# Where the score shifts of three of four token groups are computed in a cross-attention kernel, and by which engines and queues they reach their consumer

## The chip, the cores and the metric

One core of one Trainium2 chip runs the whole program. The metric is device time in microseconds (us) of one execution; beside it stands the span of the profiled execution, from its first to its last recorded instruction. The kernel works in float32 throughout; where speed matters it splits a float32 operand into an upper and a lower float32r part and multiplies the parts.

## The reference, cut to what matters

```python
# x: (16, 100, 512), ctx: (16, 722, 256); B, T, E = 16, 100, 512; M, L = 722, 256
q = x @ Wq + bq
k = ctx @ Wk + bk
v = ctx @ Wv + bv
w = softmax((q @ k.T) / sqrt(E), axis=1)      # over the 100 tokens t, not over the context rows
y = w @ v + x
out = (y - mean(y)) * rsqrt(var(y) + 1e-6) * gamma + beta
```

The softmax runs over the tokens. A score of token t and context row m is ctx[m]·G[t] plus a term that depends on the token alone, c[t] = x[t]·u + bb, with u = Wq·bk and bb = bq·bk, both scaled by 1/sqrt(E). Because the softmax is over t, this term, the score shift, cannot be left out.

## The kernel before, in words

The 16 batches are dealt with in four groups of four (400 tokens each). The start computes W = Wq·Wk (transposed) and u on TensorE from weights loaded in four parts, and then project(g) forms G for the 400 tokens of group g. From then on each batch b passes through a turn: scores_of(b) (24 matmuls into ps_S, lines 417 to 421), maxima(b) on VectorE (add the shift to the scores, then the negated maximum over tokens, lines 744 and 748), exponentials(b) on ScalarE, normaliser(b) on VectorE, probabilities(b) on GpSimd, weighted_ctx(b) (24 matmuls into ps_U, line 433), and then, for tiles of 128 output rows, values, residual and layer norm.

Every engine runs its instructions in the order written. TensorE's order is written out at lines 471 to 487: project(0), project(1), scores of batch 0, project(2), scores of 1, project(3), then turns in which scores_of(b) comes ahead of weighted_ctx(b - 2). scores_of(b) waits for S_read, that is for maxima(b - 1) to have emptied the single pair of score banks. weighted_ctx(0) waits also for the G of all four groups, the last of which ScalarE takes (take_group(3)) after exponentials(1).

The shift of a group is made in this way. VectorE multiplies the transposed tokens xT_in (feature on the partition, 400 tokens along the row) by u, one feature chunk after another: weigh_by_u, four instructions of 128x400 (lines 724 and 728). ScalarE (upper_shift, line 567) and VectorE (lower_shift, line 735) split the result. TensorE (sum_shift, lines 407 and 408) multiplies both parts by a matrix of ones, which sums over partitions and leaves the sum on all 128 of them; ScalarE (take_shift, line 571) copies it into c_rows, from which maxima reads. Nothing of it touches a DMA queue.

VectorE's order is written out at lines 827 to 869. After maxima(0) come lower_half(3) (line 715, the lower part of group 3's tokens), weigh_by_u(1), normaliser(0), maxima(1), chunk_sum(0), normaliser(1), lower_shift(1), weigh_by_u(2), maxima(2), and so on.

The loads all go through SyncE's one queue (lines 265 to 318). It issues the weights, the four groups of tokens, two batches of context in both layouts, three parameter rows, Wv and two tiles of x without a wait, and then waits in turn for buffers: next_ctxT(2) waits for the scores of batch 0 and next_ctx(2) for weighted_ctx(0). There are two buffers each for ctxT and ctx.

Of the kernel before, what the change touches and what calls it, by code (L numbers as in the profile page):

```python
# [24 lines left out]
P = 128  # L25
# [5 lines left out]
def xattn(nc, xT, x, ctxT, ctx, Wqk, Wv, bv, gamma, beta, out):  # L31
# [18 lines left out]
    with ExitStack() as stack:  # L50
        def sb(name, shape, dt=F32):
            return stack.enter_context(nc.sbuf_tensor(name, shape, dt))
# [4 lines left out]
        def sem(name):  # L57
            return stack.enter_context(nc.semaphore(name))
# [12 lines left out]
        g_bias = sb("g_bias", [P, LC])  # L71
# [16 lines left out]
        xu_hi = sb("xu_hi", [P, 2, GT], F32R)  # L88
        xu_lo = sb("xu_lo", [P, 2, GT], F32R)
# [49 lines left out]
        u_set = sem("u_set")  # L139
        gbias_set = sem("gbias_set")  # L140
# [58 lines left out]
        y = wv_in  # L199
        centred = wqT[:, 0:2, :]  # L200
# [16 lines left out]
        def tile_of(b):  # L217

            return next((j for j in range(NT) if last_batch(j) == b), None)
# [44 lines left out]
        def _(sp):  # L264
# [65 lines left out]
        def _(pe):  # L330
# [35 lines left out]
            def bias_sums():  # L366

                pe.wait_ge(wkq_step, EC)
                for c in range(LC):
                    last = nc.tensor.matmul(ps_w[:, c:c + 1], wkq[:, (EC - 1) % 2, c * P:(c + 1) * P], ones[:, 0:1],  # L370
                                            start=True, stop=True)
                last.then_inc(gbias_summed, 1)
# [26 lines left out]
            def sum_shift(g):  # L399

                pe.wait_ge(xuhi_set, g + 1)
                pe.wait_ge(xulo_set, g + 1)
                if g >= 1:
                    pe.wait_ge(c_set, g)
                else:
                    pe.wait_ge(onesr_set, 1)
                nc.tensor.matmul(ps_c[:, 0:GT], ones_r[:, :], xu_hi[:, g % 2, :], start=True, stop=False)  # L407
                nc.tensor.matmul(ps_c[:, 0:GT], ones_r[:, :], xu_lo[:, g % 2, :], start=False, stop=True).then_inc(c_summed, 1)  # L408
# [65 lines left out]
            sum_shift(0)  # L474
# [4 lines left out]
            sum_shift(1)  # L479
# [65 lines left out]
        def _(act):  # L545
# [17 lines left out]
            def upper_shift(g):  # L563
                act.wait_ge(xu_step, EC * (g + 1))
                if g >= 2:
                    act.wait_ge(c_summed, g - 1)
                nc.scalar.activation(xu_hi[:, g % 2, :], xu[:, (EC - 1) % 2, :], ACT.Copy).then_inc(xuhi_set, 1)

            def take_shift(g):
                act.wait_ge(c_summed, g + 1)  # L570
                nc.scalar.activation(c_rows[:, g * GT:(g + 1) * GT], ps_c[:, 0:GT], ACT.Copy).then_inc(c_set, 1)
# [63 lines left out]
            nc.scalar.activation(g_bias[:, :], ps_w[:, 0:LC], ACT.Copy, scale=SCALE).then_inc(gbias_set, 1)  # L635
# [3 lines left out]
            upper_shift(0)  # L639
            take_group(1)  # L640
            upper_half(3)
            take_shift(0)
            exponentials(0, 0)
            take_group(2)
            upper_shift(1)
# [5 lines left out]
            upper_shift(2)  # L651
            upper_U(0, 0)
            exponentials(2, 0)
            take_shift(1)
            value_bias(0)
            exponentials(3, 1)
            turn(4, 0)
            turn(5, 1)
            take_shift(2)
            each_turn(turn, 6, 9)  # L660
            upper_shift(3)
            turn(9, 1)
            turn(10, 0)
            take_shift(3)
            each_turn(turn, 11)
# [20 lines left out]
        def _(dve):  # L686
# [32 lines left out]
            def weigh_by_u(g, terms=tuple(range(EC))):  # L719
                if g >= 1 and 0 in terms:  # L720
                    dve.wait_ge(xulo_set, g)
                for e in terms:
                    if e == 0:
                        nc.vector.tensor_scalar(xu[:, 0, :], xT_in[:, g, 0, :], u_col[:, 0:1], bb_col[:, 0:1],
                                                ALU.mult, ALU.add).then_inc(xu_step, 1)
                    else:
                        dve.wait_ge(xu_step, EC * g + e)
                        nc.vector.scalar_tensor_tensor(xu[:, e % 2, :], xT_in[:, g, e, :], u_col[:, e:e + 1],  # L728
                                                       xu[:, (e - 1) % 2, :], ALU.mult, ALU.add).then_inc(xu_step, 1)

            def lower_shift(g):
                dve.wait_ge(xuhi_set, g + 1)
                if g >= 2:
                    dve.wait_ge(c_summed, g - 1)
                nc.vector.tensor_tensor(xu_lo[:, g % 2, :], xu[:, (EC - 1) % 2, :],
                                        xu_hi[:, g % 2, :].bitcast(F32), ALU.subtract).then_inc(xulo_set, 1)

            def maxima(b, q):
                dve.wait_ge(c_set, b // GB + 1)
# [87 lines left out]
            weigh_by_u(0)  # L827
            lower_half(2, (0,))
            lower_shift(0)
# [5 lines left out]
            weigh_by_u(1)  # L835
# [4 lines left out]
            lower_shift(1)  # L840
            weigh_by_u(2)
            maxima(2, 0)
            lower_U(0, 0)
            lower_shift(2)
# [15 lines left out]
            turn(5, 1)  # L860
            weigh_by_u(3, (0, 1))
            turn(6, 0)
            weigh_by_u(3, (2,))
            turn(7, 1)
            weigh_by_u(3, (3,))
            turn(8, 0)
            turn(9, 1)
            lower_shift(3)
            each_turn(turn, 10, B - 1)
# [181 lines left out]
```

## Time and profile before

| | us |
|---|---|
| runs, median (lowest to highest) | 143.87 (143.75 to 144.3) |
| the profiled execution's own time | 144.33 |
| its span | 142.6 |
| TensorE matmul busy | 135.5 |
| VectorE busy | 114.1 |
| ScalarE busy | 78.7 |
| GpSimd busy | 65.2 |

Busy times count the records of an engine. TensorE's loads of weights lie beside its matmuls. The profile's granted clock of TensorE over the run is 0.991 of full speed. The DMA queue of SyncE moved 34.79 of 37.33 MB.

### The profile page before, as it was taken

How to read it: one execution, taken by the hardware profiler on the slowest of the kernel's cores; microseconds unless marked ns; L12 is line 12 of the kernel's file. 1: busy time of each engine (PE TensorE's matmuls, PEld its weight loads, DVE VectorE, ACT ScalarE, POOL GpSimd, SP SyncE). 2: the span in 40 equal slices, each digit the busy share in tenths (PEclk: the TensorE clock that was granted, in tenths of full speed). 3: DMA queues.
4: the chain of work that ended last, by engine and by line, in shares of the span. 5: the costliest groups of instructions: out<-in, count | busy, mean ns of one | idle time of the engine just before them, and what ended most of it. 6: DMA issues, size and time to landing. Idle time of an engine off the chain costs nothing.

```text
span 142.6 us, 2971 instructions
## 1 busy us (share of the span) xinstructions
PE 135.5 (95%) x1046; PEld 130.9 (92%) x1046; DVE 114.1 (80%) x221; ACT 78.7 (55%) x282; POOL 65.2 (46%) x61
## 2 busy tenths in 40 slices
PE   6999999999999999989999999999999999999940
PEld 6899999999998999989999999999999999999930
DVE  0379995996997779689999987877789976797993
ACT  4167088577276924574655638474847546386320
POOL 1000000027304681734667553639486645639991
PEclk9999999999999999999999999999999999999996
DMA  4999999936077595986996979697997985635314
GB/s 148 333 397 419 423 300 381 353 156 214 11 260 255 172 390 159 353 342 163 340 319 241 334 259 375 225 336 229 303 305 247 341 291 219 219 114 183 138 43 178
DMA packets 10814, 37.33 MB, mean 262 GB/s; under 512 B 1200, under 2 KB 1456, under 8 KB 10800
## 3 DMA queue, kind: packets, MB, share of 16 engines
q1 hardware_dynamic: 9424, 34.79, 69.8%
q10 hardware_dynamic: 1376, 2.36, 4.4%
q8 instruction: 8, 0.13, 0.4%
q14 instruction: 6, 0.05, 0.1%
HBM read 33.87 MB, written 3.28 MB: 260 GB/s over the span
## 4 chain that ended last, share of the span: by engine, by line
PE 88%; POOL 6%; issue 2%; ACT 1%; DVE 0%; POOLq 0%; DVEq 0%
PE ps_S L419 29%; PE ps_U L433 26%; PE ps_Y L454 10%; PE ps_U L392 6%; PE ps_Y L392 6%; PE ps_Y L337 3%; POOL xT_in L970 2%; POOL xT_in L958 2%; PE ps_S L341 1%; POOL prob L947 1%; PE ps_w L442 1%; PE ps_U L341 1%; PE ps_c L407 1%; POOL rstd L963 1%; PE ps_c L408 1%
## 5 line engine op out<-in xcount | busy, mean ns | idle before, releaser
L578 ACT ACTIVATE expo<-scores,negmax 121x100 f32<-121x100 f32 x96 | 35.0, 366 | 28.4 <-DVE negmax L748 28.4
L419 PE MATMUL ps_S<-G,ctxT_in 128*121 128x100 f32 (+1 forms) x384 | 43.4, 269 | 0.0
L419 PEld LDWEIGHTS ps_S<-G,ctxT_in 128*121 128x121 f32 (+1 forms) x384 | 42.1, 185 | 0.0
L433 PEld LDWEIGHTS ps_U<-prob,ctx_in 121*128 121x128 f32 x336 | 39.4, 192 | 0.9
L433 PE MATMUL ps_U<-prob,ctx_in 121*128 121x100 f32 x336 | 39.6, 274 | 0.0
L947 POOL TENSOR_TENSOR prob<-expo,rinv 121x600 f32<-121x600 f32 x16 | 19.6, 1228 | 31.3 <-DVE rinv L755 31.2
L958 POOL TENSOR_TENSOR xT_in<-x_in,xT_in 128x512 f32<-128x512 f32 (+1 forms) x13 | 16.6, 1281 | 16.7 <-issue 8.6
L759 DVE TENSOR_REDUCE probsum<-prob 121x100 f32<-121x600 f32 x16 | 19.8, 1237 | 4.1 <-POOL prob L947 3.8
L963 POOL TENSOR_TENSOR rstd<-vareps,neg_half 128x1 f32<-128x1 f32 (+1 forms) x13 | 11.7, 902 | 22.9 <-DVE vareps L786 22.9
L744 DVE TENSOR_TENSOR scores<-ps_S,c_rows 121x600 f32<-121x600 f32 x16 | 12.5, 779 | 9.7 <-PE ps_S L419 6.7
L578 ACT ACTIVATION_READ_ACCUMULATOR expo<-scores,negmax 121x1 f32 x96 | 18.0, 187 | 0.0
L970 POOL TENSOR_TENSOR xT_in<-wqk,beta_rows 128x512 f32<-128x512 f32 (+1 forms) x12 | 15.3, 1282 | 2.7 <-ACT wqk L604 2.7
L604 ACT ACTIVATE wqk<-wqk,rstd 128x512 f32<-128x512 f32 (+1 forms) x12 | 8.6, 719 | 9.8 <-POOL rstd L963 7.8
L748 DVE TENSOR_REDUCE negmax<-scores 121x6 f32<-121x600 f32 x16 | 12.5, 778 | 0.5
L596 ACT ACTIVATE xT_in<-bv_rows,wsum 128x512 f32<-128x512 f32 (+1 forms) x13 | 9.4, 723 | 0.4
L777 DVE BATCH_NORM_STATS2 stats<-wv_in 128x6 f32<-128x512 f32 (+1 forms) x12 | 8.3, 692 | 0.4
L790 DVE SCALAR_TENSOR_TENSOR wqk<-wv_in,meanvar,gamma_rows 128x512 f32<-128x512 f32 (+1 forms) x11 | 8.4, 767 | 0.0
L772 DVE TENSOR_TENSOR wv_in<-ps_Y,xT_in 128x512 f32<-128x512 f32 (+1 forms) x12 | 8.2, 682 | 0.1
L454 PE MATMUL ps_Y<-Wv_hi,wq_parts 128*128 128x512 f32 (+1 forms) x22 | 7.8, 436 | 0.4 <-issue 0.4
L728 DVE SCALAR_TENSOR_TENSOR xu<-xT_in,u_col,xu 128x400 f32<-128x400 f32 x12 | 7.6, 634 | 0.4
L715 DVE TENSOR_TENSOR xT_lo<-xT_in,xT_hi 128x800 fp32r<-128x800 f32 x8 | 7.6, 984 | 0.0
L454 PE MATMUL ps_Y<-Wv_lo,wq_parts 128*128 128x512 f32 (+1 forms) x22 | 6.9, 395 | 0.0
(122 smaller groups left out, 184.4 us busy)
## 6 DMA issues: line engine op xcount, KB each, us to landing
ctx_in<-ctx SPq DMA_DIRECT2D x16, 768.0 KB, 5.1
ctxT_in<-ctxT SPq DMA_DIRECT2D x16, 722.0 KB, 4.3
xT_in<-xT SPq DMA_DIRECT2D x8, 400.0 KB, 9.1
x_in<-x SPq DMA_DIRECT2D x12, 256.0 KB, 4.4
out<-xT_in ACTq DMA_DIRECT2D x8, 256.0 KB, 4.2
wqk<-Wqk SPq DMA_DIRECT2D x4, 388.0 KB, 4.9
out<-xT_in SPq DMA_DIRECT2D x3, 256.0 KB, 2.0
wv_in<-Wv SPq DMA_DIRECT2D x1, 512.0 KB, 15.3
```

What stands on the lines that cost most here:

```text
L392: last = nc.tensor.matmul(bank[:, c, 0:GT], wpart[:, e, c * P:(c + 1) * P], xpart[:, q, e, :], start=(n == 0), stop=(n == 3 * EC - 1))
L419: last = nc.tensor.matmul(ps_scores(c)[0:rows(c), :], ctxT_in[:, q, l * M + c * MP:l * M + c * MP + rows(c)], G[:, l, bass.ds(b * T, T)], ...
L433: last = nc.tensor.matmul(ps_U[:, q, l * T:(l + 1) * T], ctx_in[0:rows(c), q, c, l * P:(l + 1) * P], prob[0:rows(c), q, c * T:(c + 1) * T] ...
L454: last = nc.tensor.matmul(ps_Y[0:tile_rows(j), q, :], upart[:, l, tokens(j)], vpart[:, l, :], start=(n == 0), stop=(n == 3 * LC - 1))
L578: last = nc.scalar.activation(expo[0:MP, q, c * T:(c + 1) * T], scores[0:MP, q, c * T:(c + 1) * T], ACT.Exp, bias=negmax[0:MP, q, c:c + 1] ...
L744: nc.vector.tensor_tensor(split_chunks(scores[0:MP, q, :]), ps_S[0:MP, :, 0:HALF * T].rearrange("p b (c t) -> p b c t", t=T), shift, ALU.a ...
L748: nc.vector.tensor_reduce(negmax[0:MP, q, :], scores[0:MP, q, :].rearrange("p (c t) -> p c t", t=T), AX.X, ALU.max, negate=True).then_inc( ...
L759: nc.vector.tensor_reduce(probsum[0:MP, batch_tokens(b)], prob[0:MP, q, :].rearrange("p (c t) -> p t c", t=T), AX.X, ALU.add).then_inc(pro ...
L947: nc.gpsimd.tensor_tensor(prob[0:MP, q, :].rearrange("p (c t) -> p c t", t=T), expo[0:MP, q, :].rearrange("p (c t) -> p c t", t=T), rinv[0 ...
L958: nc.gpsimd.tensor_tensor(resid[0:n, q, :], x_in[0:n, q, :], bvw[0:n, q, :], ALU.add).then_inc(resid_set, 1)
L963: nc.gpsimd.tensor_tensor(rstd[0:n, q:q + 1], vareps[0:n, q:q + 1], neg_half[0:n, :], ALU.pow).then_inc(rstd_set, 1)
L970: nc.gpsimd.tensor_tensor(result[0:n, q, :], scaled[0:n, q, :], beta_rows[0:n, :], ALU.add).then_inc(result_set, 1)
```

## The change

Group 0 keeps its way. For groups 1 to 3, c[t] is computed as a dot product with the token on the partition: dot_with_u(b) multiplies the 100 rows of batch b by a copy of u that stands on all partitions and sums along the row into one column of dots; shift_columns(g) adds bb. Four things are needed for it that were not there:

- u as a row on all partitions: SyncE waits for u_set, stores u_col to DRAM (512 words of 4 bytes), waits for that store, and loads it back to 128 partitions.
- x with the token on the partition: load_xrows(g), 800 KB for a group in pieces of 2 KB onto 100 partitions. It lies over xT_in, so the load of group 1 waits for the lower halves of groups 0 and 1 and for weigh_by_u, the load of group 2 for all eight lower halves, and the load of group 3 (same place as 2) for the dot products of group 2.
- bb on all partitions: a third matmul in bias_sums, and a g_bias of three columns.
- c as rows on all partitions: spread_c(g) stores 400 words of 4 bytes to DRAM, waits for the store, and loads them back to 128 partitions.

All these DMAs go on SyncE's queue. The u store with its wait and load_xrows(1) stand ahead of next_ctxT(2), load_xrows(2) and spread_c(1) between next_ctxT(2) and next_ctxT(4). VectorE has the dot products at the places of weigh_by_u. Gone are weigh_by_u, lower_shift, upper_shift, sum_shift and take_shift of groups 1 to 3. The core of the diff:

```diff
+            sp.wait_ge(u_set, EC)
+            sp.dma_start(u_words.rearrange("(c p) -> p c", p=P), u_col[:, :], allow_slow_non_contiguous=True).then_inc(u_stored, 16)
+            sp.wait_ge(u_stored, 16)
+            sp.dma_start(u_rows[:, :], u_words.partition_broadcast(P)).then_inc(u_rows_in, 16)
+            sp.wait_ge(xTlo_set, 4)
+            sp.wait_ge(xu_step, EC)
+            load_xrows(1)
             next_ctxT(2, 0)
+            sp.wait_ge(xTlo_set, 8)
+            load_xrows(2)
             next_ctxT(3, 1)
+            spread_c(1)
             next_ctxT(4, 0)
             next_ctx(2, 0)
+            sp.wait_ge(dots_set, 2 * GB)
+            load_xrows(3)
+            spread_c(2)
             for b in range(3, B + 1):
+                if b == 9:
+                    spread_c(3)
...
+            def load_xrows(g):
+                sp.dma_start(xrows[g], x[g * GB:(g + 1) * GB].rearrange("b t e -> t b e")).then_inc(xrows_in[g], 16)
+            def spread_c(g):
+                sp.wait_ge(c_cols_set, g)
+                sp.dma_start(c_words[g * GB:(g + 1) * GB, :].rearrange("b t -> t b"),
+                             c_cols[0:T, g * GB:(g + 1) * GB], allow_slow_non_contiguous=True).then_inc(c_stored, 16)
+                sp.wait_ge(c_stored, 16 * g)
+                sp.dma_start(c_rows[:, g * GT:(g + 1) * GT],
+                             c_words[g * GB:(g + 1) * GB, :].rearrange("b t -> (b t)").partition_broadcast(P)).then_inc(c_rows_in[g], 16)
...
             project(3)
             turn(2, 0)
-            sum_shift(1)
...
-            turn(4, 0)
-            sum_shift(2)
-            each_turn(turn, 5, 11)
-            sum_shift(3)
-            each_turn(turn, 11)
+            each_turn(turn, 4)
...
+            def dot_with_u(b):
+                g = b // GB
+                dve.wait_ge(xrows_in[g], 16)
+                dve.wait_ge(u_rows_in, 16)
+                nc.vector.scalar_tensor_tensor(xrows[g][:, b % GB, :], xrows[g][:, b % GB, :], 1.0, u_rows[0:T, :], ALU.mult, ALU.mult,
+                                               accum_out=dots[0:T, b:b + 1]).then_inc(dots_set, 1)
...
             lower_half(3)
-            weigh_by_u(1)
+            for b in range(1 * GB, 2 * GB):
+                dot_with_u(b)
+            shift_columns(1)
             normaliser(0, 0)
             maxima(1, 1)
             chunk_sum(0, 0)
             normaliser(1, 1)
-            lower_shift(1)
-            weigh_by_u(2)
+            for b in range(2 * GB, 3 * GB):
+                dot_with_u(b)
+            shift_columns(2)
             maxima(2, 0)
```

## Rows read from the trace of the kernel before

**Rows 1.** The page, part 1: busy time, share of span, instructions.
```profile
PE 135.5 (95%) x1046; PEld 130.9 (92%) x1046; DVE 114.1 (80%) x221; ACT 78.7 (55%) x282; POOL 65.2 (46%) x61
```
**Rows 2.** Chain that ended last, in order of time: start us, us, what.
```profile
17.99 0.34 PE ps_w L370 x4
...
35.56 2.51 PE ps_S L419 x24
38.06 2.68 PE ps_U L433 x24
...
40.95 0.38 PE ps_c L407
41.33 0.18 PE ps_c L408
41.51 2.51 PE ps_S L419 x24
...
54.89 0.21 PE ps_c L407
55.10 0.18 PE ps_c L408
...
93.89 0.29 PE ps_c L407
94.18 0.19 PE ps_c L408
```
**Rows 3.** Loads of x_in, issued at 15.5: duration ns, start us, landing.
```profile
L280 SPq DMA_DIRECT2D x_in<-x x1: 1782/1782/1782, 15.5 to 15.5; - x1
DMA to landing us min/median/max: 15.1/15.1/15.1
```
**Rows 4.** Timeline of VectorE from 26.5 us: start us, us, engine, line, what.
```profile
26.51 1.88 DVE L715 TENSOR_TENSOR xT_lo<-xT_in,xT_hi 128x800 fp32r<-128x800 f32 x2
28.31 0.49 DVE L724 TENSOR_SCALAR xu<-xT_in,u_col,bb_col 128x400 f32<-128x400 f32 x1
...
30.73 0.18 DVE L753 RECIPROCAL rall<-expsum 121x6 f32<-121x6 f32 x1
...
31.26 0.78 DVE L744 TENSOR_TENSOR scores<-ps_S,c_rows 121x600 f32<-121x600 f32 x1
...
32.07 0.78 DVE L748 TENSOR_REDUCE negmax<-scores 121x6 f32<-121x600 f32 x1
...
35.43 0.17 DVE L755 TENSOR_TENSOR rinv<-rall,mask 121x6 f32<-121x6 f32 x1
```
**Rows 5.** Load of x_in alone in the queue, issued at 130.7.
```profile
L280 SPq DMA_DIRECT2D x_in<-x x1: 328/328/328, 130.7 to 130.7; - x1
DMA to landing us min/median/max: 2.6/2.6/2.6
```
**Rows 6.** Load of ctxT_in alone in the queue, issued at 31.2.
```profile
L274 SPq DMA_DIRECT2D ctxT_in<-ctxT x1: 328/328/328, 31.2 to 31.2; - x1
DMA to landing us min/median/max: 4.1/4.1/4.1
```
**Rows 7.** Load of ctxT_in issued at 65.0, 0.4 us behind an x_in.
```profile
L274 SPq DMA_DIRECT2D ctxT_in<-ctxT x1: 1143/1143/1143, 65.0 to 65.0; - x1
DMA to landing us min/median/max: 5.8/5.8/5.8
```
**Rows 8.** The page, part 6: issues by tile, KB each, us to landing.
```profile
ctxT_in<-ctxT SPq DMA_DIRECT2D x16, 722.0 KB, 4.3
...
out<-xT_in SPq DMA_DIRECT2D x3, 256.0 KB, 2.0
```
**Rows 9.** The page, part 5: groups of VectorE, busy, mean ns.
```profile
L790 DVE SCALAR_TENSOR_TENSOR wqk<-wv_in,meanvar,gamma_rows 128x512 f32<-128x512 f32 (+1 forms) x11 | 8.4, 767 | 0.0
L728 DVE SCALAR_TENSOR_TENSOR xu<-xT_in,u_col,xu 128x400 f32<-128x400 f32 x12 | 7.6, 634 | 0.4
```
**Rows 10.** Timeline of ScalarE: group 3's G taken.
```profile
35.59 1.08 ACT L559 ACTIVATE G<-ps_U,g_bias 128x400 f32<-128x400 f32 x2 [0.42 <-PE ps_U L392]
```
**Rows 11.** Matmuls of line 341 into ps_U: ns min/median/max, starts.
```profile
L341 PE MATMUL ps_U<-wqk x4: 381/419/639, 6.4 to 7.4; 128*128 128x258 f32 x4
```

More of the change, by code:

```diff
@@ L70, in xattn @@
         u_col = sb("u_col", [P, EC])
[L71 removed]
+        g_bias = sb("g_bias", [P, LC + 1])
         bb_col = sb("bb_col", [P, 1])
@@ L87, in xattn @@
         xu = sb("xu", [P, 2, GT])
-        xu_hi = sb("xu_hi", [P, 2, GT], F32R)
-        xu_lo = sb("xu_lo", [P, 2, GT], F32R)
+        xu_hi = sb("xu_hi", [P, GT], F32R)
+        xu_lo = sb("xu_lo", [P, GT], F32R)
+        u_rows = sb("u_rows", [P, E])
+        dots = sb("dots", [P, B])
+        c_cols = sb("c_cols", [P, B])
         G = sb("G", [P, LC, B * T])
@@ L139, in xattn @@
         u_set = sem("u_set")
+        u_stored = sem("u_stored")
+        u_rows_in = sem("u_rows_in")
+        xrows_in = [None] + [sem(f"xrows_in{g}") for g in range(1, NG)]
+        dots_set = sem("dots_set")
+        c_cols_set = sem("c_cols_set")
+        c_stored = sem("c_stored")
+        c_rows_in = [None] + [sem(f"c_rows_in{g}") for g in range(1, NG)]
         gbias_set = sem("gbias_set")
@@ L199, in xattn @@
         y = wv_in
+        flat = xT_in.rearrange("p g c t -> p (g c t)")
+        xrows = [None] + [flat[0:T, at:at + GB * E].rearrange("p (b e) -> p b e", e=E) for at in (0, 2 * EC * GT, 2 * EC * GT)]
+        u_words = nc.dram_tensor("u_words", [E], F32).ap()
+        c_words = nc.dram_tensor("c_words", [B, T], F32).ap()
         centred = wqT[:, 0:2, :]
@@ L371, in bias_sums @@
                                             start=True, stop=True)
+                last = nc.tensor.matmul(ps_w[:, LC:LC + 1], ones[:, :], wkq[:, (EC - 1) % 2, L:L + 1], start=True, stop=True)
                 last.then_inc(gbias_summed, 1)
@@ L397, in project, with sum_shift @@
                 last.then_inc(G_summed, 1)
[L399 to L408, printed above, removed]
+            def sum_shift():
+                pe.wait_ge(xuhi_set, 1)
+                pe.wait_ge(xulo_set, 1)
+                pe.wait_ge(onesr_set, 1)
+                nc.tensor.matmul(ps_c[:, 0:GT], ones_r[:, :], xu_hi[:, :], start=True, stop=False)
+                nc.tensor.matmul(ps_c[:, 0:GT], ones_r[:, :], xu_lo[:, :], start=False, stop=True).then_inc(c_summed, 1)
             def scores_of(b, q):
@@ L473, in _ @@
             scores_of(0, 0)
-            sum_shift(0)
+            sum_shift()
             project(2)
@@ L561, in take_group, with upper_shift, take_shift @@
                 last.then_inc(G_set, 1)
[L563 to L571, printed above, removed]
+            def upper_shift():
+                act.wait_ge(xu_step, EC)
+                nc.scalar.activation(xu_hi[:, :], xu[:, (EC - 1) % 2, :], ACT.Copy).then_inc(xuhi_set, 1)
+            def take_shift():
+                act.wait_ge(c_summed, 1)
+                nc.scalar.activation(c_rows[:, 0:GT], ps_c[:, 0:GT], ACT.Copy).then_inc(c_set, 1)
             def exponentials(b, q):
@@ L638, in _ @@
             upper_half(2)
-            upper_shift(0)
+            upper_shift()
             take_group(1)
             upper_half(3)
-            take_shift(0)
+            take_shift()
             exponentials(0, 0)
             take_group(2)
-            upper_shift(1)
             act.wait_ge(wv_loaded, 16)
@@ L717, in lower_half @@
                                             ALU.subtract).then_inc(xTlo_set, 1)
[L719 to L736, printed above, removed]
+            def weigh_by_u():
+                nc.vector.tensor_scalar(xu[:, 0, :], xT_in[:, 0, 0, :], u_col[:, 0:1], bb_col[:, 0:1],
+                                        ALU.mult, ALU.add).then_inc(xu_step, 1)
+                for e in range(1, EC):
+                    dve.wait_ge(xu_step, e)
+                    nc.vector.scalar_tensor_tensor(xu[:, e % 2, :], xT_in[:, 0, e, :], u_col[:, e:e + 1],
+                                                   xu[:, (e - 1) % 2, :], ALU.mult, ALU.add).then_inc(xu_step, 1)
@@ new lines, in lower_shift @@
+            def lower_shift():
+                dve.wait_ge(xuhi_set, 1)
+                nc.vector.tensor_tensor(xu_lo[:, :], xu[:, (EC - 1) % 2, :], xu_hi[:, :].bitcast(F32),
+                                        ALU.subtract).then_inc(xulo_set, 1)
+            def dot_with_u(b):
[4 more added lines that the diff above has]
+                                               accum_out=dots[0:T, b:b + 1]).then_inc(dots_set, 1)
@@ L738, in maxima, with shift_columns @@
+            def shift_columns(g):
+                dve.wait_ge(dots_set, GB * g)
+                dve.wait_ge(gbias_set, 1)
+                nc.vector.tensor_scalar(c_cols[0:T, g * GB:(g + 1) * GB], dots[0:T, g * GB:(g + 1) * GB], g_bias[0:T, LC:LC + 1], None,
+                                        ALU.add).then_inc(c_cols_set, 1)
             def maxima(b, q):
-                dve.wait_ge(c_set, b // GB + 1)
+                if b < GB:
+                    dve.wait_ge(c_set, 1)
+                else:
+                    dve.wait_ge(c_rows_in[b // GB], 16)
@@ L826, in _ @@
             nc.vector.memset(ps_scores(MC - 1), 0.0).then_inc(scores_zeroed, 1)
-            weigh_by_u(0)
+            weigh_by_u()
             lower_half(2, (0,))
-            lower_shift(0)
+            lower_shift()
             lower_half(2, (1,))
@@ L859, in _ @@
             centre(1)
-            turn(5, 1)
-            weigh_by_u(3, (0, 1))
+            lower_U(2, 0)
+            normaliser(4, 0)
+            maxima(5, 1)
+            dot_with_u(12)
+            dot_with_u(13)
+            chunk_sum(4, 0)
             turn(6, 0)
-            weigh_by_u(3, (2,))
+            dot_with_u(14)
             turn(7, 1)
[L865 to L869, printed above, removed]
+            dot_with_u(15)
+            shift_columns(3)
+            each_turn(turn, 8, B - 1)
             lower_U(B - 4, 0)
```

15 lines of the change are left out of this document (2 added, 13 removed).

## The prediction

> **What bounds the kernel now.** I read the busy shares first, then the chain of waits in order of time, then the timelines of VectorE and of SyncE's queue over the first 45 us. The shares give TensorE 135.5 of 142.6 us [rows 1]; the chain runs through TensorE's matmuls, piece touching piece, from 1.1 to 126.7 us, and only the last 14 us are a tail of GpSimd, VectorE and DMA. So a matmul removed before 126.7 us is worth its length in the chain, and a wait put on TensorE anywhere before it costs its full length, since nothing later has slack to give back. The reader is to look for two things: how long the shift's matmuls are in the chain, and how late the new inputs of VectorE come when VectorE's order puts maxima(1) and maxima(2), which free the score banks for TensorE, behind them.
>
> **What goes.** On TensorE three pairs of ps_c matmuls: 0.38 + 0.18, 0.21 + 0.18 and 0.29 + 0.19, together 1.43 us [rows 2]. The third bias matmul comes in: four recorded instructions of that group take 0.34 us, so one more float32 matmul (two instructions) about 0.17 us, at 18 us [rows 2]. ScalarE loses six copies of about 0.5 us, which bound nothing. On VectorE three times four instructions of 128x400 and a lower_shift go, some 3 us a group.
>
> **What VectorE gets.** Four dot products of 100x512 and one small addition a group. The trace has no product with a sum along the row. Bounds: 0.63 us from the same operation on 400 elements, 0.77 us from it on 512 [rows 9]; four times that is 2.5 to 3.1 us. With the addition and its wait for the fourth sum (up to 0.2 us) I take 3.0 us a group, near the upper row because its length is the same. VectorE's work is thus unchanged to within half a us a group; what changes is when it may start.
>
> **When it may start.** Call D the moment at which the rows of group 1 and u on all partitions are there. VectorE arrives at 28.3 us, when lower_half(3) is done; there weigh_by_u(1) started without a wait [rows 4]. The way to D is serial on SyncE's queue:
>
> 1. SyncE is through with its unwaited loads at 15.5 + 1.8 = 17.3 us; u is ready by then. The last of these loads lands only 15.1 us after its issue, at 30.6 us [rows 3]. The queue holds a backlog of some 13 us, in order. The u store is put behind it, so it lands no sooner than 30.6 us, and SyncE waits for exactly that.
> 2. The store itself, 512 words: no row has it. From below 0 (it lands with the load ahead of it); from above the 2.0 us of a lone store of 256 KB [rows 8]. I take 1.0 us, in the middle, since it is few bytes but many pieces: 31.6 us.
> 3. Then u comes back as 256 KB and the rows of group 1 as 800 KB, one behind the other. Lone loads: 256 KB in 2.6 us, 722 KB in 4.1 us [rows 5, 6, 8], so 0.0032 us per further KB. 800 KB alone would be 4.35 us; u ahead of it adds 0.8 us. That is 5.2 us as lower end. The upper end for the 800 KB is the 5.8 us of a ctxT load that came out slow [rows 7], which makes 6.6 us. The pieces are of 2 KB on 100 partitions, not whole rows on 128; I take 5.0 for the 800 KB and 5.8 us for both.
>
> D = 30.6 + 1.0 + 0.05 + 5.8 = 37.5 us; bounds 30.6 + 0 + 5.2 = 35.8 and 30.6 + 2.0 + 6.6 = 39.2.
>
> The Trainium skill (DMA: Bandwidth & Descriptors, section on why a DMA increments its semaphore by 16 and not by 1) says that a DMA of SyncE is split over the largest number of engines up to 16 that divides the slowest dimension, so 100 partitions get ten. No row here has 100 partitions in a DMA. By it the bytes of the 800 KB would take 1.6 times as long; this is a rival below, there priced from the rows. By its specifications table transfers under 512 B read before they write; that speaks for the upper end of step 2 and for nothing else in the sum.
>
> **What waits behind it.** Behind the first dot product VectorE has shift_columns(1), normaliser(0), maxima(1), chunk_sum(0), normaliser(1), dots of group 2, maxima(2). From rows 4: the normaliser takes 31.26 - 30.73 = 0.53 us, the addition of the shift 0.81, the maximum 0.78. So S_read for the scores of batch 2 comes at D + 3.0 + 0.53 + 0.81 = D + 4.35, which is 41.85 us; TensorE stood ready for these scores at 35.56 us [rows 2]. The maximum ends at D + 5.1. From there to the end of normaliser(1) there are 2.75 us (32.85 to 35.60 in rows 4: six exponentials on ScalarE lie between); then 3.0 for the second group of dots and 0.81 for maxima(2). With 0.05 for the signal the scores of batch 3 start at D + 11.75 = 49.25 us instead of 41.51 [rows 2]: 7.75 us late. The second group's own inputs are behind ctxT(2) in the queue, 722 + 800 KB or some 4.9 us after D, and are wanted at D + 7.85: hidden, 3 us to spare. weighted_ctx(0), which must also wait for take_group(3) behind exponentials(1), starts at D + 5.1 + 2.3 + 1.1 = D + 8.5 [rows 4, 10] and ends with its sum at D + 11.4, 0.35 us ahead of the point where batch 3 waits: hidden, but only just.
>
> TensorE therefore idles from about 35.5 to 41.9 us and twice shortly after. After the scores of batch 3 I find nothing that is late: maxima(3), exponentials and probabilities all shift along. The 7.75 us contain the loss of the first ps_c pair (its 0.56 us stood ahead of 41.51) and of the bias matmul (ahead of the stall). The later two pairs give 0.39 + 0.48 = 0.87 us back.
>
> **Sum.** 7.75 - 0.87 = 6.9 us on the profiled execution, 144.33 + 6.9 = 151.2 us. This execution was 0.46 us above the median of the runs shown, so for the median 143.87 + 6.9 = 150.8 us. In short: time = 143.87 + D - 30.6. With D's bounds alone 149.1 to 152.5 us.
>
> **Edits taken at nothing, and their cover.** ctxT(2) is issued behind the rows of group 1 instead of at 23.9 us: it lands near D + 2.3, before D + 4.35; with a faster VectorE it would be the next thing late. spread_c(1) has until maxima(4), over 10 us. spread_c(2) makes SyncE wait for a small store behind ctx(2) and the rows of group 3 (768 + 800 KB, about 49.4 to 55.2 us), and holds back ctxT(5), which then lands near 60.5 us and is wanted near 62.6: cost 0, up to 2 us if small stores are slow. spread_c(3) holds ctxT(11) from 84.3 to 88 us in the old times; it is wanted at 94.4. TensorE after an idle stretch may run slower: the same matmul took 639 ns and later 381 ns at the start of the run [rows 11]. At that ratio scores(2) would last 4.2 us instead of 2.5 and end at 46.05 us, just where weighted_ctx(0) may start; cost 0, bounded by 1.0 us if weighted_ctx(0) is slow as well. That it becomes cheaper than nothing is excluded, as these are waits.
>
> **Rivals.**
> - Ten engines for the 800 KB. Their byte part, 800 x 0.0032 = 2.6 us, becomes 4.1 us; alone 5.9 us, D = 38.4 us, time 151.7 us. For it: the page's rule; against it: no row. If TensorE's slow rate costs too, 152.7.
> - Small stores are slow, 3 us and more. Then D is 2 us later and ctxT(5) is late by 1 to 2 us: 153 to 155 us. Against it: 512 words are few on 16 engines.
> - The small store overtakes the backlog. It is back at about 20 us; then the rows of group 1 are issued at 21 us when weigh_by_u(0) is done, and still have the backlog's bytes ahead: 30.6 + (800 + 256) x 0.0032 = 34 us, time 147.3 us. Against it: the loads of rows 3 land in the order of issue.
> - The other side: the inputs are there when VectorE wants them, because the whole chain of three DMAs escapes the backlog. The stall begins only where D + 11.75 passes 41.51 - 0.56, so at D = 29.2 us; below it TensorE keeps its full 1.43 - 0.17 us and the time is 142.6 us. The break-even point is D = 30.6 us, the very moment at which the last early load lands. It would take three DMAs in the time of none; only their running beside the backlog could do it.
>
> **How the numbers follow.** The forecast has 0.45 (own range 149.1 to 152.5), ten engines 0.27, slow small stores 0.11, the overtaking store 0.11, the other side 0.04; 0.02 is for a gain and loss that meet. Leaving out the end of the slow stores and part of the overtaking case the range is 147.2 to 153.8 us. A change under 0.5% (0.7 us) is what a measurement of this kernel cannot tell from none. Faster 0.04, same 0.02, slower 0.94. The likeliest time is 150.8 us.
>
> **What would show it.** In VectorE's waits a single one of about 9 us at the first dot product, ended by the DMA of xrows; the u store landing just after 30.6 us; TensorE idle some 6 us before the scores of batch 2 and again before batch 3; the ps_c group with two instructions only; VectorE's dot near 0.75 us. From the scores of batch 4 on, the distances as before, less 0.39 and 0.48 us. It is wrong if the u store lands by 20 us, if ctxT(2) and not maxima(1) releases the scores of batch 2, or if a second stall of TensorE stands later than batch 4.

## The result, and the profile after

| | before | after |
|---|---|---|
| runs, median (lowest to highest) | 143.81 (143.42 to 144.47) | 186.97 (185.63 to 187.75) |
| ratio, 95% interval | | 1.2997 (1.2957 to 1.3037) |
| span of the profiled execution | 142.6 | 185.5 |
| TensorE matmul busy | 135.5 | 142.6 |

The kernel became 43 us slower; forecast were 7, with 153.8 us as the upper end. The page of the kernel after, part 1 and the clock and DMA lines of part 2 (40 slices of 4.6 us); the first line answers to [rows 1]:

```profile
PE 142.6 (77%) x1042; PEld 137.5 (74%) x1042; DVE 115.9 (62%) x233; ACT 76.6 (41%) x276; POOL 65.3 (35%) x61
...
PEclk9999999985569978855699999999759999999997
DMA  6999991069630894159997978521998779663414
```

TensorE had four waits of 2.4 to 14.7 us and ran slower after each. Its waits in the kernel after (us in total, times, longest), and its timeline at the batches concerned (start, length, what, and in brackets the idle time ahead of it). Lines 458 and 472 are 419 and 433 of before:

```profile
PE ps_S L458 <- DMA ctxT_in<-ctxT: 20.6, 3, 11.2
PE ps_S L458 <- DVE scores L776: 15.1, 2, 14.7
```
```profile
49.99 4.63 PE L458 MATMUL ps_S<-G,ctxT_in 128*121 128x100 f32 x24 [14.65 <-DVE scores L776]
54.45 2.85 PE L472 MATMUL ps_U<-prob,ctx_in 121*128 121x100 f32 x24
...
57.92 2.74 PE L458 MATMUL ps_S<-G,ctxT_in 128*121 128x100 f32 x24 [0.41 <-DVE scores L776]
...
67.27 4.40 PE L458 MATMUL ps_S<-G,ctxT_in 128*121 128x100 f32 x24 [2.44 <-DMA ctxT_in<-ctxT]
...
86.97 4.92 PE L458 MATMUL ps_S<-G,ctxT_in 128*121 128x100 f32 x24 [11.21 <-DMA ctxT_in<-ctxT]
...
134.89 4.85 PE L458 MATMUL ps_S<-G,ctxT_in 128*121 128x100 f32 x24 [6.95 <-DMA ctxT_in<-ctxT]
```

These rows add up to the result. The scores of batch 3 start at 57.92 instead of 41.51 us [rows 2], 16.4 us late. Take off 0.87 for the two later ps_c pairs. Batches 4, 5 and 11 add waits of 2.44, 11.21 and 6.95 us, and 1.7, 2.2 and 2.1 us because 24 matmuls last 4.4 to 4.9 us instead of 2.74: 26.6 us. That makes 142.6 + 16.4 - 0.9 + 26.6 = 184.7 of 185.5 us.

What held the inputs is in the timeline of SyncE's queue in the kernel after:

```profile
16.48 0.52 SPq L335 DMA_DIRECT2D u_words<-u_col  x1
34.42 0.33 SPq L337 DMA_DIRECT2D u_rows<-u_words  x1
34.87 0.36 SPq L323 DMA_DIRECT2D xT_in<-x  x1
...
48.88 0.31 SPq L328 DMA_DIRECT2D c_words<-c_cols  x1
59.80 0.33 SPq L331 DMA_DIRECT2D c_rows<-c_words  x1
60.17 0.43 SPq L288 DMA_DIRECT2D ctxT_in<-ctxT  x1
...
62.71 0.75 SPq L328 DMA_DIRECT2D c_words<-c_cols  x1
79.94 0.35 SPq L331 DMA_DIRECT2D c_rows<-c_words  x1
80.34 0.43 SPq L288 DMA_DIRECT2D ctxT_in<-ctxT  x1
...
116.17 0.80 SPq L328 DMA_DIRECT2D c_words<-c_cols  x1
127.92 0.33 SPq L331 DMA_DIRECT2D c_rows<-c_words  x1
```

Each line 331 stands where the store before it has landed: 10.9, 17.2 and 11.7 us for 1.6 KB. And each ctxT load that TensorE later waits for is issued (line 288) only after it. Not all of this is the store's own time, as loads stand ahead of it in the queue; the first experiment takes the two apart. But in the last 5 us of the first of these stores the DMA engines show no work. Stretches of the kernel after (us, busy time and number of instructions by engine, then the granted clock, the DMA share and GB/s):

```profile
30.00:34.00 4.00, 4.00 (x27) 4.00 (x27) 0.00 (x0) 0.60 (x1) 0.00 (x0) 1.00 0.00 0
...
42.00:43.00 1.00, 0.00 (x0) 0.00 (x0) 0.00 (x0) 0.00 (x0) 0.00 (x0) 0.50 1.04 228
...
52.00:54.00 2.00, 2.00 (x12) 2.00 (x12) 0.97 (x5) 1.92 (x8) 1.30 (x2) 0.52 0.50 155
54.00:56.00 2.00, 2.00 (x20) 2.00 (x20) 2.00 (x4) 0.00 (x0) 1.04 (x1) 1.00 0.02 0
...
58.00:60.00 2.00, 2.00 (x20) 2.00 (x21) 2.00 (x3) 1.38 (x8) 0.00 (x0) 1.00 0.00 0
...
61.00:62.00 1.00, 1.00 (x7) 0.67 (x6) 0.97 (x2) 0.71 (x1) 0.15 (x1) 1.00 1.05 16
```

The reader is to see three states of the DMA engines: idle with a small store outstanding (30 to 34 and 54 to 60 us); fully busy but moving 16 GB/s (61 us, the load of c back to all partitions); and fully busy at 228 GB/s with the 2 KB pieces of the rows (42 us, with ctxT(2) behind them in the queue), where a context load of before reaches 416 (33 to 34 us). TensorE's granted clock is 0.50, its lower level of 1.2 GHz, after it had idled from 35.3 us on.

### The profile page after: what moved, and what is told of

Same layout as the page of the kernel before. It is cut to its first block, busy times and chain, and to the rows that moved or that the text cites. A ratio compares the mean times of both kernels' runs of the same rounds, so it can differ in the third digit from the quotient of the medians.

```text
span 185.5 us, 2990 instructions
## 1 busy us (share of the span) xinstructions
PE 142.6 (77%) x1042; PEld 137.5 (74%) x1042; DVE 115.9 (62%) x233; ACT 76.6 (41%) x276; POOL 65.3 (35%) x61
## 3 DMA queue, kind: packets, MB, share of 16 engines
q10 hardware_dynamic: 1376, 2.36, 3.6%
## 4 chain that ended last, share of the span: by engine, by line
DMA 44%; PE 34%; SPq 10%; POOL 5%; issue 3%; DVE 1%; ACT 1%; DVEq 0%; POOLq 0%
DMA c_words<-c_cols 21%; PE ps_S L458 15%; PE ps_U L472 13%; DMA u_words<-u_col 10%; DMA ctxT_in<-ctxT 7%; DMA xT_in<-x 6%; PE ps_Y L493 5%; SPq L291 2%; SPq L294 2%; SPq L284 2%; POOL xT_in L1006 2%; POOL xT_in L994 1%; DVE xT_in L758 1%; SPq L280 1%; POOL prob L983 1%
## 5 line engine op out<-in xcount | busy, mean ns | idle before, releaser
L458 PE MATMUL ps_S<-G,ctxT_in 128*121 128x100 f32 (+1 forms) x384 | 51.5, 299 | 35.7 <-DMA ctxT_in<-ctxT 20.6
L458 PEld LDWEIGHTS ps_S<-G,ctxT_in 128*121 128x121 f32 (+1 forms) x384 | 49.6, 214 | 36.4 <-DMA ctxT_in<-ctxT 20.9
L994 POOL TENSOR_TENSOR xT_in<-x_in,xT_in 128x512 f32<-128x512 f32 (+1 forms) x13 | 16.7, 1286 | 31.2 <-issue 20.5
L999 POOL TENSOR_TENSOR rstd<-vareps,neg_half 128x1 f32<-128x1 f32 (+1 forms) x13 | 11.7, 900 | 33.4 <-DVE vareps L818 33.4
L758 DVE SCALAR_TENSOR_TENSOR xT_in<-xT_in,u_rows 100x512 f32<-100x512 f32 x12 | 8.7, 768 | 17.9 <-DMA xT_in<-x 17.9
L787 DVE TENSOR_TENSOR rinv<-rall,mask 121x6 f32<-121x6 f32 x16 | 6.6, 412 | 0.6
```

Source lines behind the costliest of these rows:

```text
L458: last = nc.tensor.matmul(ps_scores(c)[0:rows(c), :], ctxT_in[:, q, l * M + c * MP:l * M + c * MP + rows(c)], G[:, l, bass.ds(b * T, T)], ...
L758: nc.vector.scalar_tensor_tensor(xrows[g][:, b % GB, :], xrows[g][:, b % GB, :], 1.0, u_rows[0:T, :], ALU.mult, ALU.mult, accum_out=dots[0 ...
L994: nc.gpsimd.tensor_tensor(resid[0:n, q, :], x_in[0:n, q, :], bvw[0:n, q, :], ALU.add).then_inc(resid_set, 1)
L999: nc.gpsimd.tensor_tensor(rstd[0:n, q:q + 1], vareps[0:n, q:q + 1], neg_half[0:n, :], ALU.pow).then_inc(rstd_set, 1)
```

## The experiments

Edits are against the kernel after unless another is named.

**16-byte pieces.** The same two arrays go through DRAM in the order in which they lie on the partitions, in a quarter of the pieces.

```diff
-                sp.dma_start(c_words[g * GB:(g + 1) * GB, :].rearrange("b t -> t b"), c_cols[0:T, ...], allow_slow_non_contiguous=True)
+                sp.dma_start(c_words[g], c_cols[0:T, g * GB:(g + 1) * GB])
-            sp.dma_start(u_words.rearrange("(c p) -> p c", p=P), u_col[:, :], allow_slow_non_contiguous=True)
+            sp.dma_start(u_words[:, :], u_col[:, :])
```

> The changed kernel with other layouts in DRAM: u and c are stored as they lie on the partitions, in pieces of 16 bytes (128 for u, 100 for a group's c) instead of 512 and 400 pieces of 4 bytes, and are read back with a stride by VectorE. Theory A (a small store's time grows with its number of pieces: 10.9 us for 400 pieces on an idle queue): the c store lands in 2.5 to 4 us, SyncE is held three times for 4 to 9 us instead of 11 to 17, TensorE's waits for ctxT_in fall from 20.6 us to below 6, time 160 to 168 us. Theory B (the time is the round trip through DRAM behind the queue, whatever the pieces): the c store stays at 10 us or more and the time at 185 to 188 us.

165.5 us, ratio 1.151 (1.130 to 1.173). SyncE's queue in this kernel:

```profile
16.46 0.52 SPq L334 DMA_DIRECT2D u_words<-u_col  x1
29.93 0.33 SPq L336 DMA_DIRECT2D u_rows<-u_words  x1
...
44.16 0.32 SPq L328 DMA_DIRECT2D c_words<-c_cols  x1
48.38 0.33 SPq L330 DMA_DIRECT2D c_rows<-c_words  x1
...
104.00 0.37 SPq L328 DMA_DIRECT2D c_words<-c_cols  x1
108.17 0.33 SPq L330 DMA_DIRECT2D c_rows<-c_words  x1
```

The c store takes 4.2 us instead of 10.9 and 11.7, just above the range of theory A, and TensorE's waits for ctxT_in fall from 20.6 to 2.5 us. Theory A holds. But the queue was not idle, as its expectation has it: loads stand ahead of each store. What the pieces themselves cost is read from the landing of the load just ahead, ctxT(3), in the kernel after and in this one:

```profile
L288 SPq DMA_DIRECT2D ctxT_in<-ctxT x1: 994/994/994, 37.2 to 37.2; - x1
DMA to landing us min/median/max: 17.5/17.5/17.5
...
L288 SPq DMA_DIRECT2D ctxT_in<-ctxT x1: 639/639/639, 31.6 to 31.6; - x1
DMA to landing us min/median/max: 16.6/16.6/16.6
```

In the kernel after this load lands at 54.7 us and the store at 59.8, 5.1 us later (4.1 to 4.7 in three other runs with this store); here at 48.2 and 48.4 us, 0.2 us later. The third c store lands 6.9 us behind the ctx load ahead of it, here 0.4 us. The u store lands 4.2 us behind the last early load (2.2 to 4.2 us in the five runs that have it in SyncE's queue in 4-byte pieces), here 0.2 us. So the stores in 16-byte pieces cost next to nothing beyond the loads ahead of them. With 32 pieces of 4 bytes on an engine (512 on sixteen) or 40 (400 on ten, see below) a piece costs 0.07 to 0.17 us. The c store's own part is 5 and 7 us of the 10.9 and 11.7.

**The wait moved away.** SyncE issues the c store in the same place and waits for it several loads later.

```diff
             next_ctxT(4, 0)
             next_ctx(2, 0)
+            load_c(1)
...
+                if b in (5, 10):
+                    load_c(b // 5 + 1)
```

> The changed kernel, in which SyncE issues each c store where it did but waits for it and loads c back later (behind next_ctx(2), and behind the loads of turns 5 and 10). Theory A (the 27 us beyond the first stall come from SyncE being held behind the store, so that ctxT is issued late): TensorE's waits for ctxT_in go from 20.6 us to under 2, and with them three slow starts of about 2.3 us each, so 158 to 162 us; the store itself still takes 10 us. Theory B (the queues are clogged by the added bytes and pieces, the wait only shows it): ctxT_in still lands late, TensorE still waits over 10 us for it, 175 us or more.

171.3 us, ratio 1.191 (1.180 to 1.203): between the two. Waits for ctxT_in are 9.4 us, 8.0 of them before batch 5. That load is now issued at 61.1 us, right behind the rows of group 3 and the c store, and its landing time in this run is

```profile
L288 SPq DMA_DIRECT2D ctxT_in<-ctxT x1: 1937/1937/1937, 61.1 to 61.1; - x1
DMA to landing us min/median/max: 17.2/17.2/17.2
```

as long as the store itself had taken in the kernel after. So it is not only the wait of the issuer: the load lands as late although SyncE no longer waits. That it waits for the store ahead of it in the queue is argued, as this run does not show when the store landed, and the rows of group 3 stand ahead of it too; with the store in ScalarE's queue (below) the same load took 11.8 us.

**No u store.** gamma is loaded in u's place, without a wait.

```diff
-            sp.wait_ge(u_set, EC)
-            sp.dma_start(u_words.rearrange("(c p) -> p c", p=P), u_col[:, :], ...).then_inc(u_stored, 16)
-            sp.wait_ge(u_stored, 16)
-            sp.dma_start(u_rows[:, :], u_words.partition_broadcast(P)).then_inc(u_rows_in, 16)
+            sp.dma_start(u_rows[:, :], gamma.partition_broadcast(P)).then_inc(u_rows_in, 16)
```

> The changed kernel without the u store and its wait: gamma is loaded in u's place, so the shifts of groups 1 to 3 are other numbers; every dot product and load remains. Theory A (the first stall is the serial chain store, load of u, load of rows): the rows of group 1 are issued at 21 us and, with the backlog ending near 30 us, VectorE starts the dot products at 34 to 36 us instead of 46.05; time 10 to 12 us less, 175 to 177 us. Theory B (the rows of group 1 are slow by themselves, 8 us and more of transfer): the start is not before 39 us and the time 180 us or more.

177.5 us, ratio 1.235. The dot products start at 37.23 us instead of 46.05, between the two theories and just outside each: the chain of u costs 8.8 us of start, but the rows, issued at 20.1 us, still land 4.9 us after the last of the early loads (at 32.3 us in this run).

**Rows as 96 + 4 partitions.**

```diff
+                for rows_of in (slice(0, 96), slice(96, T)):
+                    sp.dma_start(xrows[g][rows_of], x[g * GB:(g + 1) * GB, rows_of, :].rearrange("b t e -> t b e"))
```

> The changed kernel with each load of rows (800 KB on 100 partitions) cut into one of 96 partitions and one of 4. Theory A (100 partitions are put on ten of the sixteen DMA engines, 96 on all): the rows of group 1 land 2 to 3 us sooner than 11.2 us after their issue, the first stall shortens by as much, and the packets under 512 B rise by 3 x 6 + 3 x 4 = 30; time 183 to 185 us. Theory B (the rows are slow because of the load of u ahead of them or their 2 KB pieces): they land as late as before, within 0.5 us, 187 us.

183.6 us. VectorE's first dot product stands 9.9 us after the issue of u_rows (33.38 to 43.24 us) instead of 11.6: 1.8 us sooner, just under the 2 to 3 of theory A. But in the four other runs of this section with the same two loads uncut it stands 9.8 (both cures), 9.9 (16-byte pieces), 11.0 (ScalarE's queue) and 11.1 us (the wait moved away) after, and the ratio, 1.277 (1.253 to 1.300), overlaps that of the kernel after. The gain in time is therefore not shown. The number of engines is, by the packet counts (page of the kernel after, then of this one):

```profile
DMA packets 14379, 40.68 MB, mean 219 GB/s; under 512 B 3052, under 2 KB 3692, under 8 KB 14364
```
```profile
DMA packets 14409, 40.68 MB, mean 222 GB/s; under 512 B 3082, under 2 KB 3722, under 8 KB 14394
```

30 more, as forecast from ten engines for 100 partitions. The kernel after fits as well: before had 1200 = 75 DMAs x 16; 11 DMAs more make 1376, six of them on ten engines take off 36, and 512 + 3 x 400 pieces give 3052. By the Trainium skill (DMA: Bandwidth & Descriptors, section on why a DMA increments its semaphore by 16 and not by 1) the number of engines is the largest up to 16 that divides the slowest dimension; the counts agree.

**c over ScalarE's queue.** Stores and loads of c, still in 4-byte pieces, are issued by ScalarE, each load some 10 us after its store (SyncE's spread_c is gone).

```diff
             take_group(3)
+            store_c(1)
...
             value_bias(0)
+            load_c(1)
             exponentials(3, 1)
-            each_turn(turn, 4)
+            store_c(2)
+            each_turn(turn, 4, 6)
+            load_c(2)
+            each_turn(turn, 6, 9)
+            store_c(3)
+            each_turn(turn, 9, 11)
+            load_c(3)
+            each_turn(turn, 11)
```

> The changed kernel with its c stores and c loads (4-byte pieces as before) on ScalarE's DMA queue, the load issued some 10 us after its store, so that neither SyncE nor a load behind it in SyncE's queue stands behind a small store. In the run with the waits deferred on SyncE, ctxT(5) still took 17.2 us to land behind the rows and the store. Theory A (loads in the same queue stand behind the small store; another queue's store runs beside them): TensorE's waits for ctxT_in under 2 us in all, one slow start of TensorE is left, time 157 to 162 us. Theory B (the small pieces occupy the DMA engines themselves, whichever queue they come from): ctxT_in still over 10 us to landing beside the store, waits for it 6 us or more, 168 us or more.

163.6 us in the profiled execution and 169.7 in the only other one, so no ratio is given; the first is 1.6 us above the range of theory A. TensorE's waits for ctxT_in are 1.0 us, for ctx_in 1.4 us, as theory A has it; but ctxT(5) still takes 11.8 us to land, as theory B has it, and the 1.0 us is TensorE's wait for it. The start is nearly as late as in the kernel after (D, the start of the dot products, at 45.10 us for 46.05, the scores of batch 3 at 57.62 us, 16.1 us late), and 142.6 + 16.1 - 0.9 + 3.3 (these and one more wait) is 161.1 of its span of 161.7 us: little more than the first stall.

**A plain load in place of u's.** 128 different rows of x instead of one row of 2 KB read 128 times.

```diff
-            sp.dma_start(u_rows[:, :], u_words.partition_broadcast(P)).then_inc(u_rows_in, 16)
+            sp.dma_start(u_rows[:, :], x_rows[0:P, :]).then_inc(u_rows_in, 16)
```

> The changed kernel in which the load of u onto 128 partitions (2 KB of DRAM read 128 times) is replaced by a load of 128 different rows of x, the same 256 KB in the same pieces; the shifts of groups 1 to 3 are other numbers. Theory A (128 reads of the same 2 KB are slow: u_rows took 6.0 us to land and its stretch moved under 150 GB/s): it lands in about 3 us, the dot products start 2.5 to 3.5 us sooner after the u store has landed, time 183 to 185 us. Theory B (the 6 us are the start of the rows' load behind it): it lands in 5 us or more and nothing moves, 186 to 188 us.

182.3 us, ratio 1.268 (1.261 to 1.276). It lands 3.4 us after its issue instead of 6.0 (5.3 to 6.0 in the runs that read u's one row from SyncE's queue): theory A, with a time a little below its range. The dot products start 9.4 us after the u store has landed instead of 11.6; as the other runs had 9.8 to 11.6, how much of the 2.2 us this load brought is not shown.

**Both cures.** The first experiment's diff and that of "c over ScalarE's queue" together: 16-byte pieces and ScalarE's queue. With them comes the read that undoes the layout:

```diff
-                shift = c_rows[0:MP, bass.ds(b * T, T)].unsqueeze(1)...
+                row = c_rows[0:MP, (b // GB) * GT:(b // GB + 1) * GT].rearrange("p (t b) -> p b t", b=GB)[:, b % GB, :]
+                shift = row.unsqueeze(1)...
```

> Both cures together: 16-byte pieces in DRAM for u and c, and the c stores and loads on ScalarE's queue. What is left then is the first stall, which the pieces shorten to 11.7 us of VectorE, with one or two slow starts of TensorE. If the two causes are separate (a late start of the dot products, and loads held behind c stores) the time is 143.9 - 1.3 + about 11 to 13 = 153 to 156 us. If something else grows when they go (the dot products with a strided u take 1.06 us instead of 0.69, the added loads crowd the queue), 158 us or more.

164.2 us, ratio 1.142 (1.135 to 1.148): no better than either alone. It is outside the 153 to 156 us expected of two separate causes, and in the other case of the expectation, 158 us or more. TensorE has no wait for ctxT_in, but 12.8 us for VectorE and 3.5 us ahead of line 480; D is 40.0 us, and the scores of batch 3 still start at 54.9 us, 13.4 us late. The addition of the shift in this kernel (ns min/median/max, starts):

```profile
L787 DVE TENSOR_TENSOR scores<-ps_S,c_rows x16: 776/1228/1269, 24.1 to 142.0; 121x600 f32<-121x600 f32 x16
```

It was 779 ns before. The layout that spares the store pieces makes VectorE read c with a stride of four words, 0.45 us more in each of 12 batches, and u as well (1.06 us a dot product instead of 0.69). How much of the whole this is was not separated.

**Only groups 2 and 3.** From the kernel before: group 1 keeps its matmuls, u goes over ScalarE's queue from 13.6 us, rows in the gap of the queue, c in 16-byte pieces.

```diff
             next_ctxT(3, 1)
+            sp.wait_ge(xTlo_set, 8)
+            load_xrows(2)
...
             upper_half(1)
+            act.wait_ge(u_set, EC)
+            act.dma_start(u_words.rearrange("(c p) -> p c", p=P), u_col[:, :], ...).then_inc(u_stored, 16)
...
-            sum_shift(2)
-            sum_shift(3)
```

> The kernel before with only groups 2 and 3 changed: group 1 keeps its matmuls; u is stored and loaded on ScalarE's queue during the start; the rows of group 2 are loaded in the gap of the queue after ctxT(3), those of group 3 after the dot products of group 2, each as 96 + 4 partitions; c goes through DRAM in 16-byte pieces on ScalarE's queue, its load a turn or more after its store; the dot products stand in idle stretches of VectorE. Theory A (all costs of the change lie in waits of the start and of the queue, and they are avoidable): TensorE has no wait, its chain is 0.87 - 0.17 = 0.7 us shorter, 143.2 us, ratio 0.995. Theory B (the 1.6 MB of rows and the two slow broadcasts and stores crowd the DMA engines, which are busy 74% of the span): single ctx or ctxT loads come late and the time is 144.5 to 147 us.

152.0 us in the middle of four runs. Neither theory: something early costs more than B allowed. The stretches of this kernel at the u store (columns as above, only the end of each line read: clock, DMA share, GB/s) and ctxT(2):

```profile
22.00:24.00 2.00, 2.00 (x16) 2.00 (x15) 0.19 (x2) 1.47 (x3) 0.00 (x0) 1.00 1.79 112
24.00:26.00 2.00, 2.00 (x13) 2.00 (x12) 1.97 (x3) 0.49 (x3) 0.00 (x0) 1.00 0.69 24
26.00:28.00 2.00, 2.00 (x16) 2.00 (x15) 1.96 (x4) 2.00 (x11) 0.00 (x0) 1.00 0.33 22
...
L287 SPq DMA_DIRECT2D ctxT_in<-ctxT x1: 328/328/328, 22.8 to 22.8; - x1
DMA to landing us min/median/max: 15.0/15.0/15.0
```

It landed 8.4 us after its issue in the kernel before. Between 22 and 28 us the core moved 112, 24 and 22 GB/s; the kernel before moved 394, 325 and 354 there. The u store itself landed at 26.3 us.

**The u store later.** The same, with the u store at 35.6 us, behind the early loads, and the dot products of group 2 a turn later.

```diff
             upper_half(1)
-            act.wait_ge(u_set, EC)
-            act.dma_start(u_words.rearrange("(c p) -> p c", p=P), u_col[:, :], ...).then_inc(u_stored, 16)
...
             take_group(3)
             act.wait_ge(rows_in, 48)
+            act.wait_ge(u_set, EC)
+            act.dma_start(u_words.rearrange("(c p) -> p c", p=P), u_col[:, :], ...).then_inc(u_stored, 16)
```

> The kernel with only groups 2 and 3 changed, and the u store moved from 13.6 us, in the middle of the early loads, to about 37 us, where the queues are empty; u is loaded some 7 us later and the dot products of group 2 stand in turns 4 and 5. In the run before this, SyncE's loads moved only 22 to 112 GB/s between 22 and 28 us, beside the u store in ScalarE's queue. Theory A (512 small pieces hold up the DMA engines for loads of the other queue too, and that alone made that run 8 us longer): ctxT(2) lands 8 to 9 us after its issue as in the kernel before, TensorE's wait of 3.4 us before batch 2 and its slow start go, time 143.2 us if nothing else waits, up to 145 with the waits before line 477. Theory B (the loads of rows and the small stores later in the run cost as much): ctxT(2) is on time, and the time is still 147 us or more.

148.2 us, ratio 1.029 (1.024 to 1.035). ctxT(2) lands after 8.2 us, and the wait before batch 2 is gone; this much of A is shown. The slow stretch has moved along with the store: from 38 to 44 us the core moved 75, 26 and 55 GB/s, and ctxT(4), issued at 38.1 us, took 10.0 us to land instead of 4.1, without TensorE waiting for it. The time is that of theory B, 147 us or more. By the chain what is left is VectorE: the kernel before had it at 0%, here

```profile
PE 34%; DVE 28%; issue 16%; POOL 11%; DMA 4%; ACT 4%; POOLq 0%; ACTq 0%; DVEq 0%
```

**c sorted by ScalarE.** The same, with one copy a group on ScalarE that undoes the interleaving, and the dot products spread.

```diff
+            def sort_c(g):
+                act.wait_ge(c_rows_in[g], 16)
+                nc.scalar.activation(c_rows[:, g * GT:(g + 1) * GT].rearrange("p (b t) -> p b t", t=T),
+                                     c_mixed.rearrange("p (t b) -> p b t", b=GB), ACT.Copy).then_inc(c_set, 1)
```

> The last kernel again (only groups 2 and 3 changed, u store at about 36 us), with two edits. In it VectorE's addition of the shift read c with a stride of four words and took 1.23 to 1.28 us instead of 0.78 for batches 8 to 15, and four dot products stood together. Now ScalarE copies c once per group into plain order, so that VectorE reads it without a stride, and the dot products stand one or two to a turn. Theory A (the 4.5 us left were VectorE's: 8 x 0.45 for the stride, and dot products ahead of work that TensorE waits for): TensorE's waits ahead of line 477 fall from 3.3 us to under 1, VectorE leaves the chain again, time 143 to 144 us. If the added loads cost by themselves, ctx or ctxT waits show on TensorE and it stays above 145.

147.0 us, ratio 1.021 (1.016 to 1.025); 1.2 us better by the medians, with intervals that just touch, and not at the 143 to 144 of theory A. It is the other case of the expectation, above 145 us with a wait for a load, so VectorE was at most a part of the 4.5 us, and what made up the rest stays open. VectorE is out of the chain again (PE 79%), but TensorE waits 0.9 us for ctxT(4), which took 11.0 us to land beside the u store, and 2.5 us ahead of a line-478 matmul, behind three dot products, one of which took 1.63 us and pushed lower_U(3) back. The profiled execution (148.4 us) was 1.4 us above the median, so only its waits are read, not their sum.

**No shifts at all.** The kernel before without any work for the shifts of groups 1 to 3.

```diff
-            sum_shift(1)
...
-            weigh_by_u(1)
...
-                dve.wait_ge(c_set, b // GB + 1)
+                dve.wait_ge(c_set, 1)
...
-                shift = c_rows[0:MP, bass.ds(b * T, T)].unsqueeze(1)...
+                shift = c_rows[0:MP, bass.ds(b % GB * T, T)].unsqueeze(1)...
```

> The kernel before with all work on the shifts of groups 1 to 3 left out on every engine (they use the shifts of group 0): no products, no matmuls of ones, no copies, and nothing in their place. It measures what the removal alone can be worth. Theory A (TensorE's chain is all that counts up to 126.7 us): 1.43 us less than before, ratio 0.990. Theory B (VectorE or ScalarE also bounds some turns): more than 2 us less. If the removed matmuls were covered by a wait that ends no sooner, less than 0.7 us.

142.3 us, ratio 0.989 (0.985 to 0.993), 1.4 us less; 1.43 were forecast from [rows 2]. Its only waits on TensorE are those of the start. This is all that the change could have brought.

## Why the prediction was wrong

The direction and the first mechanism were right, the size was not.

- **What goes** was right: 1.4 us measured for 1.43. **What VectorE gets** was 0.61 us a dot product with 0.23 for the addition: 2.7 us for group 1, and 3.7 for group 2, where one dot product took 1.67 us, for 3.0 each.
- **What waits behind D** was right in its path: the scores of batch 3 started at D + 11.87 for D + 11.75. That the number fits so well is partly luck: the second group's dot products started 0.6 us sooner after D than reckoned (7.25 for 7.85) and took 0.7 us longer. TensorE's slow start before them (4.63 us) cost nothing, as reckoned, but its price of 4.2 us rested on a row that does not show a slow clock: the granted clock is 1.00 where the 639 ns of [rows 11] stand.
- **Step 2, the u store**, failed: 1.0 us with an upper end of 2.0. It landed at 34.4 us, 4.2 us behind the backlog (2.2 to 4.2 over the runs). The row that bounded it is of 256 KB in large pieces; 512 pieces of 4 bytes have another cost, about 0.1 us a piece on each engine.
- **Step 3, u and the rows**, failed: 5.8 us with an upper end of 6.6; measured 11.6, and 9.8 to 11.1 in four other kernels with the same two loads. Reading one 2 KB row 128 times is slow (5.3 to 6.0 us to landing, 3.4 for different rows), and the rows do go on ten engines, as the rival with 0.27 said at 0.9 us; but how the 4 to 6 us missing divide between these and the 2 KB pieces (228 GB/s) is not shown. D was 46.05 instead of 37.5 us: 8.5 us of the error.
- **Edits taken at nothing**: spread_c(1) had "until maxima(4), over 10 us", spread_c(2) 0 to 2 us, spread_c(3) was covered. This failed most: 26.6 of the 43 us. The cover was counted to the consumer of c; the loads queued behind the c store were checked for spread_c(2) and (3), but with a store of 2 to 4 us, and they had cover of 2 to 6 us against holds of 11 to 17 us. spread_c(1) was not checked for ctxT(4) at all. The prediction's own sign of being wrong, a second stall of TensorE later than batch 4, is there before batches 5 and 11.
- The rival "small stores are slow, 3 us and more" named the mechanism, at 153 to 155 us and 0.11. It was counted at 2 us in D and at 1 to 2 us for ctxT(5); it should have been counted at each of the four stores, with an upper end open, since no row read for it is of a piece of a few bytes.

With D as measured in the run with c on the other queue, and free c stores, the forecast's formula gives 143.87 + 45.10 - 30.6 = 158.4 us; that run had 163.6, and 3.3 of the 5.2 us between are its four small waits.

## What to carry to other kernels

Count a small scattered store by its pieces on one engine and not by its bytes, and then ask who is queued behind it and behind the wait for it: a round trip of 1.6 KB through DRAM held the load queue for 11 to 17 us, 5 and 7 of them the store's own in the two cases where that can be read. Where no row has such a piece, the bound is not the nearest DMA row; leave the upper end open or don't forecast the term. And measure first what the removed work is worth: here at most 1.4 us of 143.8, and the best arrangement of the new way that these runs found, 147.0 us, still lost to the old one.

## What the runs showed of the hardware

- A store in 4-byte pieces costs about 0.1 us a piece on its engine (0.07 to 0.17) while the profile's DMA share is 0.00: 512 pieces land 2.2 to 4.2 us behind the load ahead of them, 400 pieces on ten engines 4.1 to 6.9 us, 128 or 100 pieces of 16 bytes 0.2 to 0.4 us.
- Such a store in one queue slows loads in the other: 22 to 112 GB/s beside it, ctxT landing after 15.0 and 11.0 us instead of 8.4 and 4.1. When the store was moved, the slow stretch moved with it.
- 128 reads of the same 2 KB landed after 5.3 to 6.0 us, of 128 different rows after 3.4 us; reading back 1.6 KB for all partitions landed after 4.2 to 5.6 us, with the engines fully busy at 16 GB/s in one microsecond of it (61 us).
- Reading the second operand with a stride of four words took VectorE's addition of 121x600 from 0.78 to 1.23 us.
